# A fused layer on one TensorE: the product of a chunk's tokens made with 128 weight columns, or in two halves of 64

## The reference

```python
def step(state, inp):
    dA_t, dtx_t, B_t, C_t = inp
    state = state * dA_t[..., None, None] + dtx_t[..., None] * B_t[:, :, None, :]
    y_t = jnp.einsum('bhpn,bhn->bhp', state, C_t)
    return (state, y_t)
```

## Time and profile before

| what | value |
|---|---|
| time, median of 3 runs | 3392.07 us (3388.98 to 3392.81) |
| the profiled execution, its own time | 3389.2 us |
| its span, first to last instruction | 3387.5 us |
| PE busy | 3315.3 us, 98% |
| PEld busy | 2767.0 us, 82% |
| DVE busy | 2475.2 us, 73% |
| ACT busy | 1522.0 us, 45% |
| POOL busy | 1154.6 us, 34% |
| mean granted TensorE clock | 0.994 |

### The profile page before, as it was taken

How to read it: one execution, slowest core, us unless ns; L and a number is a source line. 1 busy time by engine, 2 the same in 40 slices (tenths; PEclk the granted TensorE clock), 3 DMA queues, 4 the chain that set the end, 5 groups by cost and what they waited for, 6 DMA issues and landing times.

```text
span 3387.5 us, 53697 instructions
## 1 busy us (share of the span) xinstructions
PE 3315.3 (98%) x16224; PEld 2767.0 (82%) x16224; DVE 2475.2 (73%) x3865; ACT 1522.0 (45%) x3454; POOL 1154.6 (34%) x1079
## 2 busy tenths in 40 slices
PE   7999999999999999999999999999999999999999
PEld 5787777887888888888878888888878888888887
DVE  6898898997677777777558766777755877766773
ACT  3565555554354444444225444444422544444441
POOL 3554554554223333323203332332320332333231
PEclk9899999999999999999999999999999999999999
DMA  6667676676665555555466555555547555555554
GB/s 221 234 249 258 237 250 223 240 251 251 234 214 178 185 170 187 176 179 185 159 206 211 181 181 174 187 174 181 192 156 245 168 185 174 176 186 174 181 173 156
DMA packets 183949, 672.80 MB, mean 199 GB/s; under 512 B 20864, under 2 KB 22016, under 8 KB 183168
## 3 DMA queue, kind: packets, MB, share of 16 engines
q1 hardware_dynamic: 161280, 584.91, 51.5%
q10 hardware_dynamic: 22400, 84.42, 7.1%
HBM read 532.41 MB, written 136.84 MB: 198 GB/s over the span
## 4 chain that ended last, share of the span: by engine, by line
PE 82%; DVE 10%; issue 3%; ACT 2%; DMA 1%; POOL 1%; ACTq 0%; DVEq 0%; SPq 0%; POOLq 0%
PE dense L843 23%; PE dense L845 22%; PE dense L844 22%; PE pY L927 6%; DVE conv_us L1172 3%; PE pD L947 1%; PE pX L911 1%; DMA w_hl<-w_split 1%; PE dense L880 1%; DVE xT L1180 1%; DVE w_hl L1078 1%; DVE E L1207 1%; PE pS L845 1%; PE pU L843 1%; PE pU L845 1%
## 5 line engine op out<-in xcount | busy, mean ns | idle before, releaser
L843 PE MATMUL dense<-xn_hi,w_hl 128*128 128x512 f32 x2880 | 1152.1, 400 | 29.9 <-issue 11.3
L845 PE MATMUL dense<-xn_hi,w_hl 128*128 128x512 f32 x2880 | 1127.8, 392 | 0.0
L844 PE MATMUL dense<-xn_lo,w_hl 128*128 128x512 f32 x2880 | 1126.0, 391 | 0.0
L843 PEld LDWEIGHTS dense<-xn_hi,w_hl 128*128 128x128 f32 x2880 | 544.1, 189 | 140.2 <-issue 23.0
L845 PEld LDWEIGHTS dense<-xn_hi,w_hl 128*128 128x128 f32 x2880 | 543.3, 189 | 116.8
L844 PEld LDWEIGHTS dense<-xn_lo,w_hl 128*128 128x128 f32 x2880 | 544.7, 189 | 114.2 <-issue 7.5
L1172 DVE SCALAR_TENSOR_TENSOR conv_us<-conv_in,const_g,conv_us 128x512 f32<-128x512 f32 x576 | 458.9, 797 | 13.6
L843 PE MATMUL dense<-z_hi,w_hl 128*128 128x512 f32 x1024 | 412.1, 402 | 2.9 <-DVE acc L1255 2.1
L461 POOL TENSOR_TENSOR rstd<-ssq,eps_t 128x1 f32<-128x1 f32 x128 | 40.1, 313 | 1099.7 <-ACT xD L654 1099.7
L845 PE MATMUL dense<-z_hi,w_hl 128*128 128x512 f32 x1024 | 401.4, 392 | 0.0
L437 POOL TENSOR_TENSOR xD<-x_ck,D_g 128x512 f32<-128x512 f32 x128 | 181.6, 1419 | 643.4 <-ACT x_ck L624 552.2
(11 more groups left out here) (175 smaller groups left out, 4920.5 us busy)
## 6 DMA issues: line engine op xcount, KB each, us to landing
w_hl<-w_split SPq DMA_DIRECT2D x732, 512.0 KB, 3.5
w_split<-w_hl SPq DMA_DIRECT2D x244, 512.0 KB, 3.3
cum_b<-cum_scratch ACTq DMA_DIRECT2D x128, 512.0 KB, 4.8
w_raw<-w_slots_dram SPq DMA_DIRECT2D x122, 512.0 KB, 5.1
acc<-x_tr_dram ACTq DMA_DIRECT2D x4, 2048.0 KB, 11.3
out_tr_dram<-acc ACTq DMA_DIRECT2D x16, 512.0 KB, 4.3
BC<-x_tok_dram SPq DMA_DIRECT2D x6, 512.0 KB, 4.6
conv_us<-x_tok_dram SPq DMA_DIRECT2D x6, 512.0 KB, 5.9
```

The lines of the kernel that those rows point to most:

```text
L843: nc.tensor.matmul(out, lhs[0], rhs[0], start=start, stop=False)
L844: nc.tensor.matmul(out, lhs[0], rhs[1], start=False, stop=False)
L845: return nc.tensor.matmul(out, lhs[1], rhs[0], start=False, stop=stop)
```

## The change

For every head the product is made as two matmuls in place of one. The first takes the weight columns 0 to 63 of `E[:, h, :]` and writes the partitions 0 to 63 of `pY` (the first 64 tokens of the chunk), the second takes the columns 64 to 127 and writes partitions 64 to 127. Both read the same 64 moving columns of `dtx` over all 128 partitions.

```diff
@@ -924,8 +924,9 @@
                     for h in range(HPG):
                         if h % 4 == 0:
                             pe.wait_ge(m_done, n * 2 + (h // 4 + 1))
-                        mm = nc.tensor.matmul(pY[:, h * P:(h + 1) * P], E[:, h, :], dtx[:, h * P:(h + 1) * P],
-                                              start=True, stop=True)
+                        for r in (slice(0, 64), slice(64, 128)):
+                            mm = nc.tensor.matmul(pY[r, h * P:(h + 1) * P], E[:, h, r], dtx[:, h * P:(h + 1) * P],
+                                                  start=True, stop=True)
                     mm.then_inc(s2, 1)
```

## The result

The changed kernel takes 3340.49 us (median of 4 runs, 3336.95 to 3343.42) beside 3391.31 us for the kernel before. The ratio is 0.985, with a 95% interval of 0.9833 to 0.9867: 51 us faster. The forecast was 3435 us, slower. It was wrong in its sign, and what happened is rival A, with less of a gain than its 3324 us.

A forecast was written before the change was run, and what follows sets the result against it. PE was taken to bound the kernel; a chunk goes from 1.96 to 0.32 + 0.05 + 1.79 + 0.16 = 2.32 us, +46 us over 128 chunks, less 3 hidden: 3435 us. Likeliest case's range 3420 to 3455; 8 in 10 from 3322.

The forecast's parts named there:

- rival A: In pY's product the two halves run at the same time: chunk 1.43 us, −68 us in all, 3324 us; chance 0.31.
- What bounds the kernel: PE is busy for 98% of the span, so work added to its stream lengthens the kernel almost one for one.
- The load of 128 weight columns sets the pace; a 64-column load takes about 55 ns: In pY's product a full-width pass takes 0.11 us, set by its load; load time is proportional to the columns.
- Inside the chunk's product: 32 narrow passes of pY follow one another at 0.056 us: 1.79 us, the same as 1.76 us before.
- the serial case: The forecast itself: pY's loads go one after the other at 55 ns and the crossings are paid, 3435 us; chance 0.48.
- The way in and out: Entering the narrow tile before pY costs 0.32 us plus 0.05 for the first load, leaving it 0.16 us, each chunk.
- Rival B: A load to one tile waits for the other tile's matmul in pY's product: +267 us, 3656 us; chance 0.12.
- Rival C: Nothing measurable: crossings around pY cost nothing beyond the first load's 0.05 us, 3392 to 3400 us; chance 0.09.

The follow-up runs named there:

- e1: The changed kernel with both halves of every head in the tile at column 0, writing partitions 0 to 63 of pY: 3423.17 us, ratio 1.010.
- e2: The changed kernel with all eight first halves of a chunk ahead of all eight second halves, 16 passes in a row to one tile: 3408.15 us, ratio 1.0059.
- e10: The changed kernel with heads taken four at a time, so runs of eight passes go to one tile before the other: 3372.09 us, ratio 0.9951.
- e3: The kernel before with head 7 alone made in two halves, the seven others at full width: 3408.18 us, ratio 1.0063.

## Why the prediction was wrong, step by step

- **What bounds the kernel**: right for three blocks of four. There the time fell 12 to 15 us a block where the chunks give 16. In the first block it fell 4 to 8 us, and with e1's longer chunks it didn't rise at all.
- **The load of 128 weight columns sets the pace; a 64-column load takes about 55 ns**: right. With one tile a pass takes 0.058 us (e1), against 0.056 assumed.
- **The step that failed** is "Inside the chunk's product", with the sentence that each load runs beside a matmul as now, so that the 32 passes follow one another. This holds within one tile only (e1: 3423 us). With two tiles, loads run beside loads and matmuls beside matmuls, and 32 passes take the time of 16: 0.93 us where the sum had 1.79. That term alone turned the sign. I had the mechanism as rival A with a chance of 0.31, at the right price for the chunk (1.43 us expected, 1.46 measured). The reason that I gave against it, that only every second step changes the tile, was wrong: the pairs in the trace are complete with two passes in a row to each tile. e2 and e10 show what is lost with longer runs. The reason for it, that the path into the array had room, was in the rows and deserved more weight. The absence of a row that shows two tiles said nothing about them, and I read it as if it spoke for the serial case.
- **The way in and out**: right. The last `pS` start to the first load is 0.33 us (0.32 expected), the first load adds 0.05 as expected, the way out is 0.15 (0.16 taken). By the Trainium skill (TensorEngine Tiling (Array Packing), Tiling Modes, Key Properties) a change of mode drains the engine, while a change of tile doesn't, and different tiles load and multiply in parallel. The traces agree: 0.30 to 0.35 us for the two crossings, no gap at a change of tile, pairs of loads within 0.01 us.
- **Rival B**: its rule was contradicted. The Trainium skill (TensorE: Matmul & The Clock Gate, Part 3, The mechanism) lets a load overlap a matmul in flight only where the row group differs; here all tiles use all rows, and e1 has loads beside matmuls, one every 0.058 us.
- **Rival C**: e3 rules it out. The crossings with next to none of the gain cost 20.6 us.
- **The size of rival A**: 3324 us was expected and 3340 measured. The chunk gives 4 us of this (0.50 in place of 0.53 us). The other term that was mis-sized is what the first block's other engines take back, put at nothing in that case: 13 us of 64 by the medians, and in the traces 8 to 12 in the first block alone. In the slower direction the same term works for the kernel: e1 lost 34 us where its chunks, 0.43 us longer, account for 55, and 14 of these 21 us are in the first block. Which engine is behind it is shown only in part.

## What to carry to other kernels

Where the weight load sets the pace (few moving columns, wide weights), split the weights over column tiles, and change the tile often: the loads of the tiles run at once. Two passes to a tile in a row lost nothing here, while runs of eight and sixteen overlapped only three passes at each change. The split has to pay for two changes of the array's mode, here 0.3 us, so it wants several products in a row: one head lost 21 us, four won 19, eight 51. It ends where the moving columns set the pace; four tiles brought little more than two. And it brings less where other engines are near their limit, as in the first block.

## What the runs showed of the hardware that was not expected

- Loads for two column tiles that use the same rows start less than 0.01 us apart, and the 32 passes of a chunk take as long as 16: 1.01 us of loads against 1.94 in one tile.
- A change of tile after a run of passes to one tile overlaps three of them: 28 steps of 0.058 us for 16 and 16, 31 for one tile, 1.32 us for four runs of eight.
- A change between full-width and narrow work costs at each side: 0.33 us from the last wide matmul's start (512 columns) to the first narrow load, where a wide load starts with it, and 0.15 us from the last narrow start until the next wide load.
